# A transformer's attention output product computed by halves of the tokens, ahead of the next projection

## The chip, the cores and the metric
The kernel runs on one core of a Trainium2 chip. The metric is the device time of one execution in microseconds (us); lower is better. A core has TensorE (PE: matmuls; weight loads are shown apart as PEld), VectorE (DVE), ScalarE (ACT), GpSimd (POOL) and SyncE (SP), which here only starts DMAs. Each engine runs its own program in order; they meet at semaphores. PE writes its results to PSUM, which has eight banks of 128 x 512 fp32.

## What is computed
Four batches of 512 tokens, width 256, go through four blocks of gated cross-attention and feed-forward layers. The last of these feed-forward layers is itself a transformer of depth 6, and it alone is touched by the change:

```python
for i in range(DEPTH):          # 6
    x = attn_layer(shift_tokens(x), Wqkv[i], q_scale[i], k_scale[i], Wo[i]) + x
    x = ffn_layer(shift_tokens(x), ln_g[i], ln_b[i], W1[i], b1[i], W2[i], b2[i]) + x
```

`attn_layer` has 16 heads of 64: a projection to q, k and v, l2-normalized and rotated q and k, attention of each token to a window of 64 and the window before it, and the output product `out @ Wo`. `ffn_layer` is a layer norm, a product to two halves of 682, `a * gelu(gate)`, and a product back to 256.

## The kernel before
Before 2136 us the kernel computes the first parts (`first_part`), which the change leaves alone. `last_part` computes the transformer. x stays in SBUF, transposed: 2 chunks of 128 features by 4 batches by 512 tokens. A **unit** (d, g, b) is one layer d, one group g of four heads and one batch b: 96 units. Its 512 tokens are taken as four tiles tt of 128. fp32 values are split in a high and a low fp32r part, and every large product is three matmuls (`three`, L1449).

All engines walk the same list of steps, made by `last_order` (L1214). It puts steps into **turns**; unit n puts the steps of its tile tt at turn 4n + tt + lag, so that in a steady turn each stage works on another tile:
- `qkv` (lag 0, PE L1493): 12 matmuls, six of 512 columns (q, k) and six of 256 (v). DVE rotates q and k (L1631 to L1633), then ACT squares them (L1741); this Square is what frees the first PSUM bank of `qkv` (signal `sq_act`), the copy of v (L1738) the second.
- `rot` (lag 1): DVE sums the squares (L1639), POOL adds, clamps, takes a power and scales (L1814, L1816, L1818, L1821).
- `tr` (3, PE L1501) transposes q and k; ACT copies them (L1748, L1753).
- `sc`, `ex` (4): scores (PE L1511, L1516) into the one score buffer of two banks, maximum on DVE (L1645, L1649), four exps on ACT (L1760). The next `sc` waits until they are done.
- `dv` (5, DVE L1654, L1656), `pt` (6, PE L1525, ACT L1766), `pv` (7, PE L1535, ACT L1773 to `att_hi`, DVE L1660 to `att_lo`).
- `wo` m = 0, 1 (PE L1449 with wout, one per 128 output features: 6 matmuls of 512 columns each) at turns 4n + 10 and 4n + 11; `wx` (DVE L1666), which adds the product to x, both at 4n + 11.

Within a turn the order is that of `rank` and `place` (L1264 to L1271), the same for every engine; steps without a rank have 20, and among equals the order of `put` holds, units before FFN. For PE a turn reads `sc`, (`wo` m=1), `pv`, `tr`, `pt`, FFN steps, `qkv` (30), (`wo` m=0: 31). `lq` (32) loads, casts and splits weights (DVE L1615, POOL L1810).

The FFN of batch (d, b) is laid among the turns of later units: `fo` (POOL L1826: sum for the norm, waits for the last `wx`), `fa` (PE L1553, DVE L1672), `fq` (ACT L1778, POOL L1829), `fb` (PE L1558), `fy` (L1566), `fc`, `fd` (L1786, L1688), then `hg` (gate tiles, gelu L1794), `ha` and `hm` (linear tiles; DVE L1698 multiplies, L1705 casts to `hid_hi`, L1708 takes the rest of the half-filled last tile, POOL L1838 makes `hid_lo`) and `fw`, `fx` (back to 256). In turns with t mod 64 = 2, 18, 34 and 50 PE has `ha` of one batch and `fa` of another.

PSUM banks 2 to 7 are given out by `plan` (L84): it goes through the list of steps, takes for each step that needs a bank the one that has been free longest, and makes PE wait (`left`) for the signal that freed it. So the order of the list decides which signal a step waits for. The work buffers in SBUF (`work_at`) are handled likewise; in turns 50 to 52 the buffer of the rotary L1631 is one that POOL's L1838 or L1821 frees.

Of the kernel before, what the change touches and what calls it, by code (L numbers as in the profile page):

```python
# [7 lines left out]
ALU = mybir.AluOpType  # L8
# [9 lines left out]
P = 128  # L18
# [1195 lines left out]
def last_order():  # L1214
# [4 lines left out]
    def put(t, *parts):  # L1219
        turn.setdefault(t, []).extend(parts)  # L1220
# [17 lines left out]
    for n, (d, g, b) in enumerate(units):  # L1238
        for stage, lag in (("qkv", 0), ("mv", 1), ("rot", 1), ("tr", 3), ("sc", 4), ("ex", 4), ("dv", 5), ("pt", 6), ("pv", 7)):
            for tt in range(QT):  # L1240
                put(4 * n + tt + lag, (stage, (d, g, b, tt)))
        for m in range(C):
            put(4 * n + 10 + m, ("wo", (d, g, b, m)))
            put(4 * n + 11, ("wx", (d, g, b, m)))
    for d in range(DEPTH):
        for b in range(B):
            t0 = 64 * d + 32 * (b // 2)
# [13 lines left out]
            if d == DEPTH - 1:  # L1261
                put(t0 + second[0], ("kb", b))
                put(t0 + second[2] + 1, ("fin", b))
    rank = {st: i for i, st in enumerate(("fo", "mv", "sc", "wo", "pv", "tr", "rot", "dv", "ex", "pt", "wx"))}  # L1264
    rank.update({"qkv": 30, "lq": 32})

    def place(t, p):

        if t < 0:
            return 40 if p[0] not in rank else rank[p[0]]  # L1270
        return 31 if p[0] == "wo" and p[1][3] == 0 else rank.get(p[0], 20)  # L1271

    return Order(p for t in sorted(turn) for p in sorted(turn[t], key=lambda p: place(t, p)))

# [1 line left out]
def last_part(nc, a, at, s):  # L1276
# [14 lines left out]
    with ExitStack() as p2:  # L1291
# [78 lines left out]
        def remainder(u, i):  # L1370
# [5 lines left out]
        wqkv_at = plan(order, range(2), lambda p: [p[1][1:4]] if p[0] == "lq" and p[1][0] == "q" and p[1][4] == 0 else [],  # L1376
                       lambda p: [(w, "qkv_pe") for w, u in last_use.items() if p == ("qkv", u + (QT - 1,))])
        wout_at = plan(order, range(2), lambda p: [p[1][1:4]] if p[0] == "lq" and p[1][0] == "o" else [],
                       lambda p: [(w, "add_pe") for w, u in last_use.items() if p == ("wo", u + (C - 1,))])
        key_at = use(1, [("tr", 3, [(0,)], ["kT"])], [("sc", 3, [(QT - 1,)], ["kT"], "sc_pe")])  # L1380
        val_at = use(7, [("qkv", 4, any_, ["v"])], [("pv", 4, any_, ["v"], "pv_pe")])
        mix_at = plan(order, range(8),
# [37 lines left out]
        def bank(key):  # L1420
            return psum[:, one[key][0], :]
# [57 lines left out]
        def tensor_program():  # L1479
            PE.wait_ge(S_["rt_in"], 16 + 32)  # L1480
            PE.wait_ge(S_["zeroed"], 1)
            for stage, u in order.walk():
# [54 lines left out]
                                                    start=True, stop=True)  # L1537
                    ins.then_inc(S_["pv_pe"], 1)
                elif stage == "wo":
                    d, g, b, m = u  # L1540
                    PE.wait_ge(S_["pv_dve"], at_("pv", (d, g, b, QT - 1)))
                    w = weights_of(d, g, b)
                    PE.wait_ge(S_["lq_pool"], loaded(("o",) + w, 0))
                    wh, wl = wout_hi[:, wout_at[w][0], :], wout_lo[:, wout_at[w][0], :]
                    left(one, ("wo", u), PE)
                    for k in range(2):
                        w0 = k * D + m * P
                        ins = three(bank(("wo", u)), wh[:, w0:w0 + P], wl[:, w0:w0 + P], att_hi[:, k, :], att_lo[:, k, :], k == 0, k == 1)
                    ins.then_inc(S_["add_pe"], 1)
                elif stage == "fa":  # L1550
                    PE.wait_ge(S_["fo_pool"], at_("fo", u))
# [44 lines left out]
        def vector_program():  # L1596
# [3 lines left out]
            for stage, u in order.walk():  # L1600
# [59 lines left out]
                    vector.tensor_tensor(att_lo[:, :, tok(tt)], wide(bank(("pv", u, 0))[:, 0:2 * P]), att_hi[:, :, tok(tt)].bitcast(F32),  # L1660
                                         ALU.subtract).then_inc(S_["pv_dve"], 1)
                elif stage == "wx":
                    d, g, b, m = u
                    V.wait_ge(S_["add_pe"], at_("wo", u))
                    V.wait_ge(S_["xs_pool"], at_("xs", (d, b)))
                    vector.tensor_tensor(tokens(b, m), bank(("wo", u)), tokens(b, m), ALU.add).then_inc(S_["add_dve"], 1)  # L1666
                elif stage == "fa":
                    d, b = u
                    V.wait_ge(S_["fa_pe"], at_("fa", u))
# [52 lines left out]
        def scalar_program():  # L1722
            for stage, u in order.walk():
# [44 lines left out]
                elif stage == "pv":  # L1768
                    d, g, b, tt = u
                    A.wait_ge(S_["pv_pe"], at_("pv", u))  # L1770
                    if tt == 0 and (d, g, b) != (0, 0, 0):
                        A.wait_ge(S_["add_pe"], order.nth["wo", u[:3] + (0,)] - 1)
                    scalar.activation(att_hi[:, :, tok(tt)], wide(bank(("pv", u, 0))[:, 0:2 * P]), ACT.Copy).then_inc(S_["pv_act"], 1)  # L1773
                elif stage == "fq":
                    A.wait_ge(S_["fa_dve"], at_("fa", u))
                    left(work_at, ("n1", u), A)
                    for c in range(C):
                        ins = scalar.activation(buf(f"n{c}", u), buf(f"c{c}", u), ACT.Square)  # L1778
                    ins.then_inc(S_["fa_act"], 1)
                elif stage == "fc":  # L1780
                    d, b = u
                    A.wait_ge(S_["fy_dve"], at_("fy", u))
                    if batch_nth(u):
                        A.wait_ge(S_["ha_pe"], HT // 2 * batch_nth(u))
                    for c in range(C):
                        ins = scalar.activation(xn_hi[:, c, :], buf(f"c{c}", u), ACT.Identity, bias=vec(f"ln_b{d}", c))  # L1786
                    ins.then_inc(S_["fc_act"], 1)
                elif stage == "hg":
                    d, b, j = u
                    A.wait_ge(S_["hg_pe"], at_("hg", u))  # L1790
                    for i, key in zip(tiles_of(u), half_tiles(stage, u)):
                        r, lo = rows(i), P // 2 if i == HT - 1 else 0
                        left(work_at, ("g", (d, b), i), A)
                        ins = scalar.activation(buf("g", (d, b), i)[0:r, :], bank(key)[lo:lo + r, :], ACT.Gelu, bias=vec(f"b1g{d}", i)[lo:lo + r, :])  # L1794
                    ins.then_inc(S_["hg_act"], 1)

        def gpsimd_program():
            pool_step = at.pool_step
            G.wait_ge(S_["zeroed"], 1)
            for stage, u in order.walk():  # L1800
# [20 lines left out]
                    gpsimd.tensor_tensor(k, k, bc(st[:, 12:16], 2, LHD), ALU.mult).then_inc(S_["rot_pool"], 1)  # L1821
                elif stage == "fo":
                    d, b = u
                    G.wait_ge(S_["add_dve"], at_("wx", (d, last_group(b), b, C - 1)))
                    left(work_at, ("n0", u), G)
                    gpsimd.tensor_tensor(buf("n0", u), tokens(b, 0, 0), tokens(b, 1, 1), ALU.add).then_inc(S_["fo_pool"], 1)  # L1826
                elif stage == "fq":
# [246 lines left out]
```

## Time and profile before

| | us |
|---|---|
| median of 3 runs | 4802.01 (4800.52 to 4803.77) |
| profiled execution | 4805.08 |
| its span, first to last instruction | 4803.7 |
| PE busy | 4591.3 (96%) |
| DVE busy | 3584.6 (75%) |
| ACT busy | 3135.8 (65%) |
| POOL busy | 2594.6 (54%) |
| last part: first to last `sc` | 2136.0 to 4719.2 |

The page sums up one profiled execution. The timeline lists instructions in order of time; neighbours of one kind are merged (x4), the end of a matmul is modelled and overlaps its successor's start, so the length of PE's steps is read from start to start. In brackets stands the idle time of the engine before the instruction and who ended it. DVE and POOL instructions overlap their successors by some 0.08 us.

### The profile page before, as it was taken

How to read it: one execution, taken by the hardware profiler on the slowest of the kernel's cores; microseconds unless marked ns; L12 is line 12 of the kernel's file. 1: busy time of each engine (PE TensorE's matmuls, PEld its weight loads, DVE VectorE, ACT ScalarE, POOL GpSimd, SP SyncE). 2: the span in 40 equal slices, each digit the busy share in tenths (PEclk: the TensorE clock that was granted, in tenths of full speed). 3: DMA queues.
4: the chain of work that ended last, by engine and by line, in shares of the span. 5: the costliest groups of instructions: out<-in, count | busy, mean ns of one | idle time of the engine just before them, and what ended most of it. 6: DMA issues, size and time to landing. Idle time of an engine off the chain costs nothing.

```text
span 4803.7 us, 92378 instructions
## 1 busy us (share of the span) xinstructions
PE 4591.3 (96%) x34598; PEld 2927.6 (61%) x34664; DVE 3584.6 (75%) x6388; ACT 3135.8 (65%) x7744; POOL 2594.6 (54%) x2346
## 2 busy tenths in 40 slices
PE   6999999999999999969999999999999999999998
PEld 2333333334444343337788888888888888888886
DVE  4767766766675857858888887888888888887885
ACT  3666566556455556557777777777777777777773
POOL 3322211212121222148888788787888887887873
PEclk8999999999999999989999999999999999999999
DMA  5323323332222323212111111111111111111110
GB/s 121 66 50 62 75 42 60 71 63 47 57 40 60 68 41 74 40 34 54 41 41 35 41 40 36 42 39 37 39 44 39 39 36 41 40 36 38 39 44 31
DMA packets 178924, 233.05 MB, mean 49 GB/s; under 512 B 29648, under 2 KB 121424, under 8 KB 178256
## 3 DMA queue, kind: packets, MB, share of 16 engines
q1 hardware_dynamic: 178480, 227.14, 21.0%
q8 instruction: 277, 4.54, 0.4%
q14 instruction: 167, 1.37, 0.1%
HBM read 150.09 MB, written 32.51 MB: 38 GB/s over the span
## 4 chain that ended last, share of the span: by engine, by line
PE 66%; DVE 12%; ACT 8%; POOL 7%; issue 5%; DMA 1%; SPq 0%; another core or an unknown queue 0%; DVEq 0%; ACTq 0%; POOLq 0%
PE psum L1449 13%; PE psum L1493 11%; PE psum L541 5%; PE psum L527 5%; PE psum L506 5%; PE psum L1535 3%; PE psum L1501 3%; PE psum L488 2%; DVE maxes L731 2%; PE psum L1516 2%; PE psum L1525 2%; POOL stats L1818 2%; PE psum L530 2%; ACT lprobs L1760 2%; PE psum L496 2%
## 5 line engine op out<-in xcount | busy, mean ns | idle before, releaser
L941 ACT ACTIVATE probs<-psum 128x1024 f32<-128x1024 f32 x610 | 621.6, 1023 | 449.2 <-PE psum L527 259.7
L731 DVE TENSOR_REDUCE maxes<-psum 128x1 f32<-128x1024 f32 x512 | 618.1, 1216 | 278.0 <-PE psum L506 274.2
L1818 POOL TENSOR_TENSOR stats<-stats,minus_half 128x8 f32<-128x8 f32 x384 | 687.6, 1791 | 32.0
L1760 ACT ACTIVATE lprobs<-psum,small_stats,stats 128x128 f32<-128x128 f32 x1536 | 690.3, 480 | 20.9 <-DVE small_stats L1649 19.9
L1493 PE MATMUL psum<-wqkv_hi,xs_hi 128*128 128x512 f32 (+1 forms) x1536 | 546.6, 356 | 16.4 <-POOL xs_lo L1805 15.2
L1814 POOL TENSOR_TENSOR lwork<-lwork 128x512 f32<-128x512 f32 x384 | 505.1, 1315 | 74.7 <-DVE lwork L1633 74.6
L527 PE MATMUL psum<-stack 98*128 98x512 bf16 x1536 | 502.8, 384 | 25.9 <-DVE maxes L731 12.2
L1493 PE MATMUL psum<-wqkv_lo,xs_hi 128*128 128x512 f32 (+1 forms) x1536 | 519.3, 338 | 0.0
L1493 PE MATMUL psum<-wqkv_hi,xs_lo 128*128 128x512 f32 (+1 forms) x1536 | 519.0, 338 | 0.0
L506 PE MATMUL psum<-stack 96*128 96x512 bf16 x1536 | 473.3, 385 | 33.2 <-ACT probs L938 10.0
L728 DVE CUSTOM_DVE_ANT_0 psum<-psum,mask_by_query 128x1024 f32<-128x1024 f32 x256 | 314.8, 1231 | 217.8 <-PE psum L506 216.2
L1741 ACT ACTIVATE lwork<-psum 128x512 f32<-128x512 f32 x384 | 231.4, 603 | 358.0 <-DVE lwork L1633 357.9
L1631 DVE TENSOR_TENSOR lwork<-psum,rotary 128x512 f32<-128x512 f32 x384 | 262.5, 684 | 210.9 <-PE psum L1493 101.9
L541 PE MATMUL psum<-probs,values 128*32 128x512 f32 x3072 | 412.9, 610 | 0.8 <-ACT probs L941 0.8
L1656 DVE TENSOR_TENSOR lprobs<-lprobs,small_stats 128x512 f32<-128x512 f32 x384 | 380.0, 990 | 13.1
L527 PEld LDWEIGHTS psum<-stack 98*128 98x128 bf16 x1536 | 137.8, 100 | 390.0 <-issue 221.7
L1760 ACT ACTIVATION_READ_ACCUMULATOR lprobs<-psum,small_stats,stats 128x1 f32 x1536 | 348.9, 227 | 0.0
L1089 POOL TENSOR_TENSOR attn<-attn,sums 128x512 f32<-128x512 f32 x48 | 62.3, 1298 | 502.5 <-DVE sums L764 502.5
L1493 PEld LDWEIGHTS psum<-wqkv_hi,xs_hi 128*128 128x128 f32 x1536 | 291.4, 190 | 62.1 <-issue 20.9
L1493 PEld LDWEIGHTS psum<-wqkv_lo,xs_hi 128*128 128x128 f32 x1536 | 291.6, 190 | 43.7 <-issue 5.3
L1493 PEld LDWEIGHTS psum<-wqkv_hi,xs_lo 128*128 128x128 f32 x1536 | 290.8, 189 | 32.7
L506 PEld LDWEIGHTS psum<-stack 96*128 96x128 bf16 x1536 | 147.6, 98 | 261.6 <-ACT probs L938 27.8
(244 smaller groups left out, 11398.0 us busy)
## 6 DMA issues: line engine op xcount, KB each, us to landing
mixed_vals<-vals SPq DMA_DIRECT2D x672, 64.0 KB, 2.0
stack<-k_parts SPq DMA_DIRECT2D x288, 128.0 KB
staged<-in_quads SPq DMA_DIRECT2D x144, 256.0 KB, 3.0
k_parts<-parts SPq DMA_DIRECT2D x48, 384.0 KB, 2.9
stack<-q_parts SPq DMA_DIRECT2D x288, 64.0 KB
staged<-in_w SPq DMA_DIRECT2D x54, 256.0 KB, 3.0
ctx<-in_ctxT SPq DMA_DIRECT2D x24, 512.0 KB, 5.2
q_parts<-parts SPq DMA_DIRECT2D x24, 384.0 KB, 3.2
```

The lines of the kernel that those rows point to most:

```text
L506: ins = tensor.matmul(ps[:, i, :], q[0:STACK, h, qt * P:(qt + 1) * P], k[0:STACK, h, i * S:(i + 1) * S], start=True, stop=True)
L527: ins = tensor.matmul(ps[:, i, :], ky[0:STACK + 2, h, kt * P:(kt + 1) * P], q[0:STACK + 2, h, :], start=True, stop=L != 1)
L541: ins = tensor.matmul(bank(acc)[32 * h:32 * h + 32, :], values[:, kt, 4 * g + h, :], pr, start=kt == 0, stop=kt == KT - 1)
L728: ins = vector.tensor_tensor_reduce(out=scores, in0=scores, in1=masks_q[:, qt * S2:(qt + 1) * S2], scale=1.0, scalar=-3e38, op0=ALU.add, o ...
L731: ins = vector.tensor_reduce(to, pair(("M", u)), AX.XY, ALU.max)
L941: scalar.activation(probs[:, i % 6, :, :], pair(("E", u)), ACT.Exp).then_inc(S_["E_act"], 1)
L1449: ins = tensor.matmul(ps, l, r, start=first and n == 0, stop=last and n == 2)
L1493: ins = tensor.matmul(to, x_[:, c, b % 2, tok(tt)], w_[:, c * COLS + lo:c * COLS + hi], start=c == 0 and n == 0, stop=c == C - 1 and n == 2)
L1656: vector.tensor_tensor(pr, pr, bc(rc, 2, P), ALU.mult).then_inc(S_["dv_dve"], 1)
L1760: ins = scalar.activation(pr[:, h, :], scores(u)[:, h % 2, h // 2, :], ACT.Exp, bias=st[:, 4 + h:5 + h], scale=y[:, h:h + 1], accum_out=st ...
L1814: gpsimd.tensor_tensor(t1, t1, t2, ALU.add)
L1818: pool_step(gpsimd.tensor_tensor(st[:, 8:16], st[:, 0:8], minus_half[:, :], ALU.pow))
```

## The change
The output product of a unit is cut by tokens instead of by output features. `wo` of half 0 or 1 computes both 128-feature chunks for 256 tokens: 12 matmuls of 256 columns, into the two halves of one bank. Half 0 is put at turn 4n + 10, half 1 at 4n + 11, both without a rank (20), so between `pt` and `qkv`, ahead of the FFN's steps of the same turn. Each half is added to x one turn later (`wx` at 4n + 11 and 4n + 12), with one DVE instruction over both chunks. `wo` of half h waits for `pv` of tile 2h + 1 only; ACT, before it overwrites `att_hi` of tile 0 or 2, waits for `wo` of the half that it overwrites. `fo` moves from the first to the last rank of the ranked steps, since the last `wx` of a batch can now be in its turn.

```diff
@@ last_order
-        for m in range(C):
-            put(4 * n + 10 + m, ("wo", (d, g, b, m)))
-            put(4 * n + 11, ("wx", (d, g, b, m)))
+        for half in range(2):
+            put(4 * n + 10 + half, ("wo", (d, g, b, half)))
+            put(4 * n + 11 + half, ("wx", (d, g, b, half)))
...
-    rank = {st: i for i, st in enumerate(("fo", "mv", "sc", "wo", "pv", "tr", "rot", "dv", "ex", "pt", "wx"))}
+    rank = {st: i for i, st in enumerate(("mv", "sc", "pv", "tr", "rot", "dv", "ex", "pt", "wx", "fo"))}
...
-        return 31 if p[0] == "wo" and p[1][3] == 0 else rank.get(p[0], 20)
+        return rank.get(p[0], 20)
@@ tensor_program
                 elif stage == "wo":
-                    d, g, b, m = u
-                    PE.wait_ge(S_["pv_dve"], at_("pv", (d, g, b, QT - 1)))
+                    d, g, b, half = u
+                    PE.wait_ge(S_["pv_dve"], at_("pv", (d, g, b, 2 * half + 1)))
...
-                    for k in range(2):
-                        w0 = k * D + m * P
-                        ins = three(bank(("wo", u)), wh[:, w0:w0 + P], wl[:, w0:w0 + P], att_hi[:, k, :], att_lo[:, k, :], k == 0, k == 1)
+                    these = slice(2 * half * P, 2 * (half + 1) * P)
+                    for m in range(C):
+                        for k in range(2):
+                            w0 = k * D + m * P
+                            ins = three(bank(("wo", u))[:, 2 * m * P:2 * (m + 1) * P], wh[:, w0:w0 + P], wl[:, w0:w0 + P],
+                                        att_hi[:, k, these], att_lo[:, k, these], k == 0, k == 1)
@@ vector_program
-                    vector.tensor_tensor(tokens(b, m), bank(("wo", u)), tokens(b, m), ALU.add).then_inc(S_["add_dve"], 1)
+                    x = at.X[:, :, b, PAD + 2 * half * P:PAD + 2 * (half + 1) * P]
+                    vector.tensor_tensor(x, wide(bank(("wo", u))), x, ALU.add).then_inc(S_["add_dve"], 1)
@@ scalar_program
-                    if tt == 0 and (d, g, b) != (0, 0, 0):
-                        A.wait_ge(S_["add_pe"], order.nth["wo", u[:3] + (0,)] - 1)
+                    if tt % 2 == 0 and (d, g, b) != (0, 0, 0):
+                        A.wait_ge(S_["add_pe"], order.nth["wo", u[:3] + (tt // 2,)] - 2)
```

The release of the output weights and the wait of `fo` name the last half instead of the last chunk.

## Rows read from the trace of the kernel before

**Rows 1.** The page, its head and part 1: busy us, share, instructions
```profile
span 4803.7 us, 92378 instructions
...
PE 4591.3 (96%) x34598; PEld 2927.6 (61%) x34664; DVE 3584.6 (75%) x6388; ACT 3135.8 (65%) x7744; POOL 2594.6 (54%) x2346
```

**Rows 2.** The page, part 5: count, busy us, mean ns, idle before it
```profile
L1493 PEld LDWEIGHTS psum<-wqkv_hi,xs_hi 128*128 128x128 f32 x1536 | 291.4, 190 | 62.1 <-issue 20.9
```

**Rows 3.** Timeline of PE in two plain turns (42, 43): start us, length us
```profile
3039.71 0.30 PE L1511 MATMUL psum<-band_bias,ident_b 64*64 64x256 bf16 x4
...
3043.32 0.28 PE L1493 MATMUL psum<-wqkv_hi,xs_hi 128*128 128x256 f32 x1
3043.44 0.28 PE L1493 MATMUL psum<-wqkv_lo,xs_hi 128*128 128x256 f32 x1
...
3044.03 0.40 PE L1449 MATMUL psum<-att_hi,wout_hi 128*128 128x512 f32 x1
...
3045.20 0.39 PE L1449 MATMUL psum<-att_hi,wout_lo 128*128 128x512 f32 x1
3045.51 0.30 PE L1511 MATMUL psum<-band_bias,ident_b 64*64 64x256 bf16 x4
...
3046.18 0.50 PE L1449 MATMUL psum<-att_hi,wout_hi 128*128 128x512 f32 x1
...
3051.70 0.30 PE L1511 MATMUL psum<-band_bias,ident_b 64*64 64x256 bf16 x4
```

**Rows 4.** Timeline of ACT, end of turn 43: the last exp's read
```profile
3051.32 0.23 ACT L1760 ACTIVATION_READ_ACCUMULATOR lprobs<-psum,small_stats,stats 128x1 f32 x1
```

**Rows 5.** Timeline of PE: turn 48 (bound by PE) and turn 56
```profile
3271.24 0.30 PE L1511 MATMUL psum<-band_bias,ident_b 64*64 64x256 bf16 x4
...
3278.38 0.30 PE L1511 MATMUL psum<-band_bias,ident_b 64*64 64x256 bf16 x4
...
3328.18 0.30 PE L1511 MATMUL psum<-band_bias,ident_b 64*64 64x256 bf16 x4
...
3335.72 0.30 PE L1511 MATMUL psum<-band_bias,ident_b 64*64 64x256 bf16 x4
```

**Rows 6.** Timeline of PE in turns 50 to 52, up to turn 53's start
```profile
3285.86 0.30 PE L1511 MATMUL psum<-band_bias,ident_b 64*64 64x256 bf16 x4
...
3293.91 0.30 PE L1511 MATMUL psum<-band_bias,ident_b 64*64 64x256 bf16 x4
...
3300.10 0.30 PE L1511 MATMUL psum<-band_bias,ident_b 64*64 64x256 bf16 x4
...
3301.88 0.60 PE L1525 MATMUL psum<-ident,lprobs 128*128 128x128 f32 x4
...
3304.22 0.50 PE L1449 MATMUL psum<-hid_hi,w_hi 128*128 128x512 f32 x1 [0.57 <-ACT lwork L1741]
...
3308.81 0.30 PE L1511 MATMUL psum<-band_bias,ident_b 64*64 64x256 bf16 x4
```

**Rows 7.** Timeline of DVE, POOL and ACT in the same turns
```profile
3290.03 1.39 DVE L1698 SCALAR_TENSOR_TENSOR lwork<-psum,vecs,lwork 128x512 f32<-128x512 f32 x2
...
3292.22 1.07 POOL L1821 TENSOR_TENSOR lwork<-lwork,stats 128x256 f32<-128x256 f32 x1
...
3293.25 1.28 POOL L1838 TENSOR_TENSOR hid_lo<-lwork,hid_hi 128x512 fp32r<-128x512 f32 x1
3294.66 0.69 DVE L1631 TENSOR_TENSOR lwork<-psum,rotary 128x512 f32<-128x512 f32 x1 [0.53 <-POOL hid_lo L1838]
...
3296.05 0.60 ACT L1741 ACTIVATE lwork<-psum 128x512 f32<-128x512 f32 x1 [3.03 <-DVE lwork L1633]
...
3302.18 0.69 DVE L1631 TENSOR_TENSOR lwork<-psum,rotary 128x512 f32<-128x512 f32 x1 [1.48 <-POOL lwork L1821]
```

**Rows 8.** Timeline of POOL and DVE in turn 34
```profile
3622.21 1.46 POOL L1838 TENSOR_TENSOR hid_lo<-lwork,hid_hi 128x512 fp32r<-128x512 f32 x1
3622.56 1.66 DVE L1708 TENSOR_TENSOR hid_hi<-lwork,hid_hi 42x512 fp32r<-42x512 f32 x1
```

More of the change, by code:

```diff
@@ L1378, in last_part @@
         wout_at = plan(order, range(2), lambda p: [p[1][1:4]] if p[0] == "lq" and p[1][0] == "o" else [],
-                       lambda p: [(w, "add_pe") for w, u in last_use.items() if p == ("wo", u + (C - 1,))])
+                       lambda p: [(w, "add_pe") for w, u in last_use.items() if p == ("wo", u + (1,))])
         key_at = use(1, [("tr", 3, [(0,)], ["kT"])], [("sc", 3, [(QT - 1,)], ["kT"], "sc_pe")])
@@ L1662, in vector_program @@
                 elif stage == "wx":
-                    d, g, b, m = u
+                    d, g, b, half = u
                     V.wait_ge(S_["add_pe"], at_("wo", u))
                     V.wait_ge(S_["xs_pool"], at_("xs", (d, b)))
-                    vector.tensor_tensor(tokens(b, m), bank(("wo", u)), tokens(b, m), ALU.add).then_inc(S_["add_dve"], 1)
+                    x = at.X[:, :, b, PAD + 2 * half * P:PAD + 2 * (half + 1) * P]
+                    vector.tensor_tensor(x, wide(bank(("wo", u))), x, ALU.add).then_inc(S_["add_dve"], 1)
                 elif stage == "fa":
@@ L1823, in gpsimd_program @@
                     d, b = u
-                    G.wait_ge(S_["add_dve"], at_("wx", (d, last_group(b), b, C - 1)))
+                    G.wait_ge(S_["add_dve"], at_("wx", (d, last_group(b), b, 1)))
                     left(work_at, ("n0", u), G)
```

## Prediction

> **What bounds the kernel now.** I read the page first. TensorE (PE) is busy 96% of 4803.7 us, GpSimd (POOL), VectorE (DVE) and ScalarE (ACT) far less [rows 1]; that is a mean over two parts, and the change touches only the last one, from 2136 us on. So I went to the timeline of that part and cut it into turns at each first score matmul (L1511). There are 384 turns: `qkv` loads `wqkv_hi` weights four times a turn, 1536 times in all [rows 2]. I numbered each turn t as `last_order` does and name it by t mod 64; equal numbers recur once per layer and their lengths repeat within 0.03 us in the five full layers, so one stands for all.
>
> A unit (layer, head group, batch) touches two neighbouring turns with its output product, t mod 4 = 2 ("first": `wo` m=0, behind `qkv`) and 3 ("second": `wo` m=1, between `sc` and `pv`). Outside the FFN's ends all 72 first turns last 5.80 us and all 73 second ones 6.19, though both hold the same matmuls [rows 3]. In between the reader should see a PE that never rests: these turns are bound by PE's instruction stream. The rest of the layer has turns of 7.13 to 7.14 us when only PE binds [rows 5] and a few in which PE waits for another engine, and those decide this case.
>
> **Part 1: the product by halves.** Removed per unit: 12 matmuls of 512 columns. Added: 24 of 256 columns and 12 more weight loads. The six 512-column ones of `wo` start 1.17 / 5 = 0.234 us apart, the 256-column ones of `qkv` 0.12 (0.1185 over all six) [rows 3], each with its own load: 12 x 0.234 = 2.81 against 24 x 0.1185 = 2.84 us, +0.03 a unit: nothing. The load takes 0.19 us by itself [rows 2] but is hidden at this spacing. The Trainium skill, "TensorE: Matmul & The Clock Gate", Part 3, says that a weight load overlaps a running matmul only when the row groups differ; all loads here use all rows. By its figures (107 ns a load, 109 and 216 ns a matmul, an estimate) a unit would pay 24 x 216 - 12 x 323 = 1.3 us more, 125 us in all; the row speaks against it, since load and matmul together start every 118 ns.
> DVE's two additions stay 128x512 each, one per half; nothing is added to any DMA queue and SP's order is unchanged. The first addition comes a turn earlier relative to the second; both lie inside a DVE that waits in plain turns. Cost nothing; without cover 0.65 us each.
>
> **Part 2: second turns.** `wo` between `sc` and `pv` costs them twice. The stream restarts: 0.11 us at `wo`'s own start, about 0.09 before `pv`. And `pv` 1.4 us late makes all of ACT late: its last exp read ends 3051.55, and the next `sc`, which needs the one score buffer, starts only at 3051.70, 0.28 behind the last `qkv` matmul's slot instead of 0.09 [rows 3, 4]. Both go: `wo` behind `pt` joins the stream of `qkv`. What is late next is PE itself, so the second turn becomes as long as the first, 5.80. Gain 73 x 0.386 = 28.2 us. First turns keep 5.80: `wo` only swaps places with `qkv`.
>
> **Part 3: turns that wait because the second turn was late.** The ACT and DVE work of a second turn now ends over 1 us earlier and one addition leaves it. Turn 56 loses 0.40 us to a bank that the Square of the last `qkv` (L1741) frees, 7.54 against 7.14 [rows 5]. The same 0.4 stands in turns 9, 24, 25, 41, 57 (some behind the gelu's table load), 33 turns in all: 13.2 us. Turns 17 and 49 lose 0.33 (11 turns, 3.6), turn 33 0.16 (5, 0.8). I expect all gone: 17.6 us. In the first half of layer 0, without FFN, turns of 5.3 us wait likewise (estimate 3), and in the tail one half less stands between the last attention and the last norm: 6 x 0.234 = 1.4. Sum of parts 2 and 3: **50.2 us gained**, 40 to 55.
>
> **Part 4: the three turns at the end of each FFN.** Turns 50 to 52 (and 2 to 4, 18 to 20, 34 to 36; 21 triples) are bound by DVE and POOL. Two things get worse.
> (a) In turn 50 `wo` now stands ahead of `ha`, the FFN's last linear tile. `hm` on DVE (L1698) waits for `ha`: today it starts 4.17 us into the turn [rows 6, 7]. Then: `pt` ends 2.13, `wo` 1.49, five spacings 1.17, 0.51 to DVE: 5.3. Queued behind it on DVE are the casts, L1708, two L1672, and the rotary L1631.
> (b) The banks are dealt out first in, first out in program order. I followed that list through the old and the new order. In turn 51 it is `tr` (PE 2.9 us into the turn) that takes the bank freed by the last Square; now it is `pt`, due at 1.78. In turn 52 it is the second `fw` tile, due 3.4; now `pt` at 1.78. So everything behind `pt` (`wo`, `fw`, `fb`, `qkv`) waits for Square.
> Working, from the start of turn 50. L1698 runs 5.3 to 6.7. POOL's L1821 stands at 6.4, so the first cast ends at 7.3; the second holds DVE until 7.65; POOL's L1838, freed by the first cast, starts at 7.6 and takes 1.28 [rows 7]; L1708 comes behind it and is shut out until 8.8. That is what happens in turn 34 today: L1838 first, and L1708 takes 1.66 us, not 0.69 [rows 8]. The Trainium skill, "SBUF — State Buffer", Who interferes with whom, says so: an instruction with two SBUF inputs is fully blocked by a GpSimd one that started first. L1708 ends 9.45, the pair of L1672 10.7, L1631 starts 10.64 instead of 8.80. Square is done and seen by PE 2.05 later (1.39 + 0.60 + 0.06): `pt` goes at 12.69, which is 4.64 into turn 51; behind it 4.0 remain (0.36 + 1.49 + 2.16): turn 52 starts at 16.7, today 14.24 [rows 6]. The next L1631 follows 7.52 us behind the last as today, bound by POOL: 18.16; Square lets `pt` go at 20.21, 3.5 into turn 52. Behind `pt` today's turn has 8.71 - 1.78 - 0.74 (the wait that ends at 3304.22) = 6.2: turn 53 starts at 26.4, today 22.95. Cost 3.45.
> Eleven triples (18, 50) at 3.4, five (2, where `hm` is late already, at 4.6) at 3.3, five (34, no weight cast) at 2.7: **67 us lost**.
> Both ends: were DVE not late at all, (b) alone would cost 1.6, 1.6 and 1.4, 33 us; with `hm` late but L1708 ahead of L1838, L1631 starts at 9.55, a triple costs 2.2, 1.9 and 2.3, 45 us; with one more blocked operation a triple, 80. I take 67, because the order of requests that I work out is the one of rows 8.
> `fo` moves to the end of POOL's turn: it comes 4 us later, still before `fa` a turn on, and it lets `rot` go first. Nothing.
>
> **Sum.** 67.4 - 50.2 = +17.2 us. The profiled execution took 4805.08 us (span 4803.7): 4822.3. The median of the runs is 4802.01, 3.07 lower: **4819.2**. About 0.2%, 9.6 us, is what a measurement can tell from no change.
>
> **Rivals.** 1. Faster: PE's stream wins. If Square in turns 51 and 52 is not later than today, because DVE's and POOL's queues have slack that I don't see, only 33 us are lost and gains of up to 55 stand: 4780 to 4785. The place is L1631 of turn 50; it decides at a start of about 9.1 instead of 10.64. For it: plain turns are bound by PE without doubt. Against it: L1631 there waits for POOL today, and DVE has no idle time in that turn. Chance 0.25. 2. No change: `hm` is late but L1708 slips in ahead of L1838; 45 - 50 = -5: 4797. For it: the two requests lie within 0.1 us of each other in two of the four triples. Chance 0.2. 3. Weight loads show after all: 12 x 0.19 x 96 = up to 219 us, 4900 and more; rows 3 speak against it. Chance 0.02. 4. The change doesn't do what it says, since banks or PE order keep second turns long: no gain in part 2, 4845. Chance 0.05; the new order of PE reads straight from the code.
>
> **How the numbers follow.** My forecast, slower by 17, has 0.48. Range 4783 to 4842: the ends of the loss (33, 80) with the ends of the gain. Slower by over 9.6 us: 0.48 less its low edge, plus rivals 3 and 4: 0.52. Within: 0.23. Faster: 0.25. Slower and faster nearly balance, since the result is a difference of two sums of 50 to 70 us; the likeliest case alone spans 4808 to 4835.
>
> **What would show it.** Right: second turns of 5.8 us; 7.14 in turns 9, 24, 25, 56, 57; turns 51 and 52 of about 8.7 and 9.7 us where they were 6.19 and 8.71, with `pt` (L1525) released by ACT L1741 in both; L1698 of turn 50 at 5.3; L1708 near 1.7 us. Wrong: `pt` of turns 51, 52 near 1.8 us; `qkv`'s or `wo`'s 256-column spacing above 0.13; second turns still above 6.

## The result and the profile after

The changed kernel takes 4837.66 us, the median of 4 runs (4837.12 to 4839.79), against 4802.3 before: 1.0072 of the time, 95% interval 1.006 to 1.0084. It is slower by 35.4 us, where I had forecast 17.2. The time lies inside the range, near its upper end of 4842, the sign is right, and the forecast size is half of what came.

The head of the page of the changed kernel (busy us, share, instructions; compare [rows 1]):

```profile
span 4838.5 us, 94725 instructions
...
PE 4592.6 (95%) x35816; PEld 3028.4 (63%) x35816; DVE 3614.6 (75%) x6388; ACT 3165.8 (65%) x7744; POOL 2598.6 (54%) x2346
```

PE is busy 1.3 us longer and the span is 34.8 us longer: the loss is waiting, not work. Cutting both traces into turns at the first score matmul (L1511) shows where. Each row of this table is a sum over turns in us, worked out from the starts. Turns are named as in the prediction, by t mod 64; a "triple" is the three turns at the end of an FFN:

| turns | count | before | after | difference | forecast |
|---|---|---|---|---|---|
| the triples at the FFN's ends with the turn behind them (2 to 5, 18 to 21, 34 to 37, 50 to 53), from turn 50 of layer 0 on | 85 | 642.9 | 712.8 | +69.9 | +67.4 |
| 8 and 40 | 11 | 79.8 | 89.4 | +9.6 | 0 |
| second turns (t mod 4 = 3) | 65 | 402.1 | 381.7 | -20.4 | -25.1 |
| first turns (t mod 4 = 2) | 65 | 377.3 | 379.2 | +2.0 | 0 |
| other turns, 9, 24, 25, 41, 49, 56, 57 among them | 121 | 879.4 | 860.9 | -18.5 | -17.6 |
| before turn 40 of layer 0 | 36 | 201.7 | 197.2 | -4.5 | -6.1 |
| tail | | 84.6 | 81.2 | -3.4 | -1.4 |

(The forecast of 28.2 us for 73 second turns is split here: 65 x 0.386 = 25.1, and 3.1 with the 3 us for layer 0.)

PE in a second turn of the changed kernel (turn 43; start us, length us), which answers [rows 3]. `wo` is the stream that starts at 3253.23:

```profile
3251.09 0.30 PE L1511 MATMUL psum<-band_bias,ident_b 64*64 64x256 bf16 x4
...
3253.23 0.36 PE L1449 MATMUL psum<-att_hi,wout_hi 128*128 128x256 f32 x1
3253.43 0.28 PE L1449 MATMUL psum<-att_lo,wout_hi 128*128 128x256 f32 x1
...
3254.62 0.28 PE L1449 MATMUL psum<-att_hi,wout_lo 128*128 128x256 f32 x1
...
3256.93 0.30 PE L1511 MATMUL psum<-band_bias,ident_b 64*64 64x256 bf16 x4
```

The turn is 5.84 us long instead of 6.19. Behind the first, the matmuls of 256 columns start (3254.62 - 3253.43) / 10 = 0.119 us apart.

PE in turns 50 to 52 of the changed kernel, which answers [rows 6]; turn 51 starts at 3305.33, turn 52 at 3315.39:

```profile
3305.33 0.30 PE L1511 MATMUL psum<-band_bias,ident_b 64*64 64x256 bf16 x4
...
3308.20 0.63 PE L1501 MATMUL psum<-ident,lwork 128*128 128x128 f32 x4 [1.51 <-DVE lwork L1676]
3310.09 1.09 PE L1525 MATMUL psum<-ident,lprobs 128*128 128x128 f32 x4 [1.26 <-ACT lwork L1745]
...
3312.47 0.41 PE L1449 MATMUL psum<-att_lo,wout_hi 128*128 128x256 f32 x1
3312.68 0.35 PE L1449 MATMUL psum<-att_hi,wout_lo 128*128 128x256 f32 x1
...
3315.39 0.30 PE L1511 MATMUL psum<-band_bias,ident_b 64*64 64x256 bf16 x4
...
3317.58 0.63 PE L1525 MATMUL psum<-ident,lprobs 128*128 128x128 f32 x4 [0.26 <-ACT lwork L1745]
...
3323.68 0.30 PE L1511 MATMUL psum<-band_bias,ident_b 64*64 64x256 bf16 x4
```

`tr` (L1501) waits for the bank that L1676 frees, and `pt` (L1525) waits for the Square (L1745, before L1741) in both turns, as forecast. DVE and POOL beside it, turn 50's end, which answers [rows 7] (L1702, L1712, L1634, L1825, L1842 are L1698, L1708, L1631, L1821, L1838 of before):

```profile
3302.56 1.40 DVE L1702 SCALAR_TENSOR_TENSOR lwork<-psum,vecs,lwork 128x512 f32<-128x512 f32 x2 [0.98 <-PE psum L1449]
...
3305.09 1.65 DVE L1712 TENSOR_TENSOR hid_hi<-lwork,hid_hi 42x512 fp32r<-42x512 f32 x1
...
3307.97 0.69 DVE L1634 TENSOR_TENSOR lwork<-psum,rotary 128x512 f32<-128x512 f32 x1
```

```profile
3303.51 1.26 POOL L1825 TENSOR_TENSOR lwork<-lwork,stats 128x256 f32<-128x256 f32 x1
3304.74 1.45 POOL L1842 TENSOR_TENSOR hid_lo<-lwork,hid_hi 128x512 fp32r<-128x512 f32 x1
```

Turn 50 starts at 3297.25. L1702 comes 5.31 us into it, held up by PE; POOL's L1842 starts at 7.49, L1712 behind it at 7.84 and takes 1.65 us; L1634 starts at 10.72.

Turn 8 holds what I had not looked at. PE in turn 8 (start 3006.93), the first `hg` tile:

```profile
3006.93 0.30 PE L1511 MATMUL psum<-band_bias,ident_b 64*64 64x256 bf16 x4
...
3010.19 0.47 PE L1449 MATMUL psum<-xn_hi,w_hi 128*128 128x512 f32 x1 [0.88 <-ACT lwork L1745]
```

### The profile page after: what moved, and what is told of

It is laid out like the page before. It is cut to its first block, busy times and chain, and to the rows that moved or that the text cites. A ratio compares the mean times of both kernels' runs of the same rounds, so it can differ in the third digit from the quotient of the medians.

```text
span 4838.5 us, 94725 instructions
## 1 busy us (share of the span) xinstructions
PE 4592.6 (95%) x35816; PEld 3028.4 (63%) x35816; DVE 3614.6 (75%) x6388; ACT 3165.8 (65%) x7744; POOL 2598.6 (54%) x2346
## 4 chain that ended last, share of the span: by engine, by line
PE 71%; DVE 10%; POOL 9%; ACT 5%; issue 3%; DMA 1%; SPq 0%; DVEq 0%; ACTq 0%; POOLq 0%
PE psum L1449 14%; PE psum L1493 12%; PE psum L541 5%; PE psum L527 5%; PE psum L506 5%; PE psum L1535 3%; PE psum L1501 3%; PE psum L1525 3%; PE psum L1516 2%; PE psum L488 2%; DVE maxes L731 2%; POOL stats L1822 2%; PE psum L530 2%; PE psum L496 2%; POOL lwork L1818 2%
## 5 line engine op out<-in xcount | busy, mean ns | idle before, releaser
L1822 POOL TENSOR_TENSOR stats<-stats,minus_half 128x8 f32<-128x8 f32 x384 | 677.1, 1763 | 32.0
L1493 PE MATMUL psum<-wqkv_hi,xs_hi 128*128 128x512 f32 (+1 forms) x1536 | 535.2, 348 | 16.9 <-POOL xs_lo L1809 15.8
L1634 DVE TENSOR_TENSOR lwork<-psum,rotary 128x512 f32<-128x512 f32 x384 | 264.0, 688 | 311.1 <-PE psum L1493 256.6
L1745 ACT ACTIVATE lwork<-psum 128x512 f32<-128x512 f32 x384 | 229.9, 599 | 263.7 <-DVE lwork L1636 258.1
L1659 DVE TENSOR_TENSOR lprobs<-lprobs,small_stats 128x512 f32<-128x512 f32 x384 | 390.0, 1016 | 13.1
L1742 ACT ACTIVATE vals<-psum 128x256 f32<-128x256 f32 x384 | 149.2, 389 | 362.7 <-PE psum L1493 362.2
```

Of the source, the lines that this page charges most:

```text
L1493: ins = tensor.matmul(to, x_[:, c, b % 2, tok(tt)], w_[:, c * COLS + lo:c * COLS + hi], start=c == 0 and n == 0, stop=c == C - 1 and n == 2)
L1659: vector.tensor_tensor(pr, pr, bc(rc, 2, P), ALU.mult).then_inc(S_["dv_dve"], 1)
L1822: pool_step(gpsimd.tensor_tensor(st[:, 8:16], st[:, 0:8], minus_half[:, :], ALU.pow))
```

## The experiments

Ten kernels ran. Theory: the loss is made of two things that work together in turns 50 to 52, a late `hm` (part 4a) and the bank of the Square going to `pt` (4b), and the second one also makes turns 8 and 40 longer. Rivals: one of the two alone; DVE's and POOL's own chain; the cost of the 256-column matmuls. All times are medians; the ratio is to runs of the kernel before on the same chip, 4801.5 to 4806.0 us. A difference of two medians from different chips can therefore be off by up to 5 us; what a turn costs is compared within the traces.

**e1_swap: the other order of handing back.**

```diff
-            return [(p + (i,), sem) for i, sem in enumerate(LEAVES.get(stage, ()))]
+            return [(p + (i,), sem) for i, sem in reversed(list(enumerate(LEAVES.get(stage, ()))))]
```

> The changed kernel, with one thing else: `qkv`'s two PSUM banks are handed back in the other order, first the one that the copy of v (`qkv_act`) frees, then the one that the Square (`sq_act`) frees. Nothing is moved in any engine's program; only which bank a step gets, and so which signal it waits for. In turns 51 and 52 `pt` gets the bank of the copy, and `wo` (turn 51) or the second `fw` tile (turn 52) that of the Square; in turns 8 and 40 the first `hg` tile gets that of the copy. Theory (both the late `hm` and the dealing of the banks cost): turn 50's L1634 stays at 10.6 to 10.8 us, since `hm` is still late; in turn 51 `wo` waits in place of `pt`, 0.36 us less; turn 52 waits at `fw` as in the kernel before, so its end comes 4.6 us behind the Square instead of 6.2: a triple gets 1.6 us shorter, 21 x 1.6 = 34 us, and turns 8 and 40 go back to 7.13 or 7.17 us, 10 us: 4794 us (4785 to 4803). Rival A (the dealing alone costs): all 70 + 10 us come back, 4758. Rival B (DVE's and POOL's own chain sets the triples, whoever waits on PE): only turns 8 and 40 come back, 4828.

Measured: 4797.2 us, ratio 0.9987 (0.9979 to 0.9996). Turns 8 and 40 are 7.13 us again (-10.9 us over 11 turns), and the triples lose 41.0 us instead of 69.9. L1634 of turn 50 stays at 10.72 us. The theory's two terms are there; the triples gave back 28.9 us instead of 34. What is missing is in a few turns. PE in turn 19 and in turn 51 of this kernel, which hold the same steps:

```profile
3067.62 0.30 PE L1511 MATMUL psum<-band_bias,ident_b 64*64 64x256 bf16 x4
...
3070.48 0.63 PE L1501 MATMUL psum<-ident,lwork 128*128 128x128 f32 x4 [1.51 <-DVE lwork L1676]
...
3072.28 0.57 PE L1449 MATMUL psum<-att_hi,wout_hi 128*128 128x256 f32 x1 [0.73 <-ACT lwork L1745]
...
3073.08 0.41 PE L1449 MATMUL psum<-att_hi,wout_hi 128*128 128x256 f32 x1
3073.29 0.41 PE L1449 MATMUL psum<-att_lo,wout_hi 128*128 128x256 f32 x1
```

```profile
3290.65 0.63 PE L1501 MATMUL psum<-ident,lwork 128*128 128x128 f32 x4 [1.51 <-DVE lwork L1676]
...
3292.45 0.39 PE L1449 MATMUL psum<-att_hi,wout_hi 128*128 128x256 f32 x1 [0.73 <-ACT lwork L1745]
...
3293.26 0.28 PE L1449 MATMUL psum<-att_hi,wout_hi 128*128 128x256 f32 x1
3293.38 0.28 PE L1449 MATMUL psum<-att_lo,wout_hi 128*128 128x256 f32 x1
```

The busy times and the granted clock (the number behind POOL's) of those turns:

```profile
3067.60:3077.50 9.90, 7.66 (x69) 6.70 (x68) 7.97 (x14) 5.14 (x17) 6.20 (x6) 0.83 0.06 15
...
3287.80:3296.10 8.30, 6.06 (x69) 5.22 (x68) 7.96 (x14) 4.69 (x17) 4.68 (x5) 1.00 0.06 16
```

Both turns idle for 1.51 and 0.73 us, but in turn 19 the matmuls behind run at the lower clock level (1.2 GHz), 0.21 us apart instead of 0.12. Turn 19 takes 9.92 us, turn 51 8.39; the turns behind them, 7.87 and 8.41, take 0.54 of that back. So 1.0 us is lost here. Turn 19 does so in four of the five full layers (9.86 to 9.92 us) and in one not (8.39), turn 51 in none of six. Turn 35 does it in one layer, 9.50 us instead of 7.98, and nothing gives that back. Together this is 5 us, the gap between 34 and 28.9.

**e2_wo_behind_ffn: `wo` no longer ahead of `ha`.**

```diff
-    rank.update({"qkv": 30, "lq": 32})
+    rank.update({"wo": 21, "qkv": 30, "lq": 32})
```

> The changed kernel with `wo` at rank 21: behind the FFN's steps of its turn, ahead of `qkv`. The banks' dealing in turns 51 and 52 stays as in the changed kernel (`pt` gets the Square's). Theory: `ha` is computed 1.5 us earlier again, L1702 starts 4.17 us into turn 50 instead of 5.3, L1634 at 8.8 instead of 10.7, and only the loss that the banks bring is left, 1.6 us a triple instead of 3.4: 21 x 1.8 = 37 us come back, turns 8 and 40 (no `wo` in them) stay at 8.0 to 8.2: 4800 us (4792 to 4808). Rival A (the late `hm` has no part in it): 4838, L1634 may move but turn 51 stays above 10 us. Rival B (the late `hm` is all of it): 70 us come back, 4768.

Measured: 4801.0 us, 0.9994 (0.9985 to 1.0003), and the triples lose 35.2 us, half of 69.9. DVE in turn 50 (start 3281.91) of this kernel:

```profile
3286.17 1.39 DVE L1702 SCALAR_TENSOR_TENSOR lwork<-psum,vecs,lwork 128x512 f32<-128x512 f32 x2
...
3288.26 0.68 DVE L1712 TENSOR_TENSOR hid_hi<-lwork,hid_hi 42x512 fp32r<-42x512 f32 x1
...
3290.80 0.69 DVE L1634 TENSOR_TENSOR lwork<-psum,rotary 128x512 f32<-128x512 f32 x1 [0.53 <-POOL hid_lo L1842]
```

With `ha` ahead of `wo`, L1702 starts 4.26 us into the turn, L1712 takes 0.68 us again, and L1634 stands at 8.89. `pt` still waits for the Square, 0.99 us in turn 51, 1.50 in turn 52: turn 52 is 9.54 us. This is what the banks cost by themselves.

**e3_both: the two edits together.**

> Both edits together: `wo` behind the FFN's steps, and `qkv`'s banks handed back with the copy's first. Theory: L1634 of turn 50 at 8.8 us, the Square seen by PE at 10.85; in turn 51 `pt` is free to go, `wo` waits some 0.6 us for the Square; in turn 52 the second `fw` tile waits at 18.4 us as in the kernel before, so the triple is as long as there (22.95 us from 50 to 53). Turns 8 and 40 at 7.13 to 7.17. All of the 70 + 10 us come back and the 45 us gained elsewhere stay: 4758 us (4752 to 4766). If the two causes overlapped (each edit alone already brings all), e1 and e2 alone would stand there too. If the triples were lengthened by something else (the weight loads of the 256-column matmuls, the two additions of 128x512), this one would stay above 4790.

Measured: 4755.9 us, 0.9902 (0.9887 to 0.9917). The triples are 2.4 us longer than before instead of 69.9, turns 8 and 40 1.3 us shorter. The causes add up: e1 gives 40.4 us back, e2 36.6, both together 81.8. The 4.8 us more than the sum are about the 5 us that the clock takes in e1; in e3's trace the granted clock is full in all the triples. What is left of the waits (PE, turn 51 and turn 52):

```profile
3274.82 0.38 PE L1449 MATMUL psum<-att_hi,wout_hi 128*128 128x256 f32 x1 [0.46 <-ACT lwork L1745]
...
3282.34 0.50 PE L1449 MATMUL psum<-hid_hi,w_hi 128*128 128x512 f32 x1 [0.25 <-ACT lwork L1745]
```

**b_swap: the kernel before with e1's edit alone.**

> The kernel before, with `qkv`'s banks handed back in the other order and nothing else. It tests part 3: turns 9, 24, 25, 41, 56 and 57, 0.4 us longer than PE's own 7.13, wait for the Square's bank. If so, they fall to 7.13 to 7.17 us here too, with the second turns still 6.19: 33 x 0.4 = 13 us, and in turn 52 the second `fw` tile gets the copy's bank and `fb` the Square's, 0.57 us earlier x 21 = 12 us at most: 4785 us (4777 to 4791). If instead those turns wait because the second turn's ACT work is late, whatever the bank, nothing moves: 4802. e3 less this one is then what the output product by halves is worth by itself: second turns 20 to 28 us.

Measured: 4785.2 us, 0.9963 (0.995 to 0.9975), the time forecast, but not wholly from where it was forecast. Turns 17, 24, 33, 49 and 56 fall to 7.13 or 7.14; turns 9, 25, 41 and 57 do not (7.61, 7.93, 7.59, 7.93 in most layers; 25 and 57 had been 7.54): PE in turn 57 waits at `pt` for the bank of the gelu, which stands behind its table load on ACT. PE there:

```profile
3326.58 0.63 PE L1525 MATMUL psum<-ident,lprobs 128*128 128x128 f32 x4 [0.60 <-ACT lwork L1794]
```

So part 3's turns waited for two things: some for the Square's bank (the swap frees them), some for a late ACT (the swap does not help, and the change does: 7.13 in all four). The triples became 14.7 us shorter than in the kernel before, and part 3's turns only 3.0: the sum of 4785 came out by luck. With the same handing back on both sides, the output product by halves behind the FFN's steps (e3) is worth 4785.2 - 4755.9 = 29.3 us.

**e4_rest_first: DVE's L1712 and POOL's L1842 never together.**

```diff
+                            if i == HT - 2:
+                                G.wait_ge(S_["rest_dve"], batch_nth(u) + 1)
```

> The changed kernel with one wait more: for a batch's last pair of tiles POOL starts L1842 only when DVE's L1712 is done, so the two never run together. `hm` stays late, the banks are dealt as in the changed kernel. Theory (of the 1.8 us by which L1634 is late in turn 50, 1.1 come from `ha` behind `wo`, the rest from L1712 being shut out by L1842): L1712 takes 0.69 us instead of 1.65 and ends at 8.3, L1842 runs 8.4 to 9.7, L1634 starts at 9.7 instead of 10.7; a triple gets 1.0 us shorter, 21 us in all: 4816 us (4808 to 4822). Rival A (the shutting out costs nothing, since L1634 waits for a work buffer in any case): 4838 or, as L1842 itself comes later, up to 4845. Rival B (the price of the changed kernel is mostly this shutting out): under 4800.

Measured: 4823.5 us, 1.0046 (1.0032 to 1.0059): 14 us of the 35 come back, fewer than the 21 expected and above the range's end. DVE and POOL in turns 50 and 51 (50 starts at 3289.66):

```profile
3297.50 0.69 DVE L1712 TENSOR_TENSOR hid_hi<-lwork,hid_hi 42x512 fp32r<-42x512 f32 x1
...
3299.74 0.69 DVE L1634 TENSOR_TENSOR lwork<-psum,rotary 128x512 f32<-128x512 f32 x1 [0.24 <-POOL hid_lo L1844]
```

```profile
3298.33 1.27 POOL L1844 TENSOR_TENSOR hid_lo<-lwork,hid_hi 128x512 fp32r<-128x512 f32 x1 [1.15 <-DVE hid_hi L1712]
```

L1712 takes 0.69 us instead of 1.65, 0.96 less, but L1634 is only 0.64 us earlier (10.08 into turn 50), since now it waits 0.24 us for the work buffer that POOL frees. L1634 stood at 8.89 in e2, so the changed kernel has it 1.83 us late. At least 0.64 of that, 0.64 x 21 = 13 us, is the shutting out, and at most 1.19 a triple comes from `ha` alone; e4's own wait makes POOL later, so it does not divide the two exactly.

**e5_cols256 and e9_cols128: the cut alone, in the old places.**

```diff
-                    for k in range(2):
+                    for c in range(0, 4 * P, 256):          # e9: 128
+                        for k in range(2):
...
+                            ins = three(bank(("wo", u))[:, c:c + 256], wh[:, w0:w0 + P], wl[:, w0:w0 + P],
+                                        att_hi[:, k, c:c + 256], att_lo[:, k, c:c + 256], k == 0, k == 1)
```

> The kernel before with each of `wo`'s matmuls of 512 columns cut in two of 256, in the old places (between `sc` and `pv`, and behind `qkv`): 24 matmuls and 24 weight loads a unit instead of 12 and 12, nothing moved. It measures part 1 alone. By the spacing of rows 3 (0.1185 against 0.234 us): 96 x 0.03 = 3 us more, 4805 (4801 to 4810). By the rule that a load is not hidden behind a matmul on the same rows, 1.3 us a unit: 4927.

> As e5, with `wo`'s matmuls cut in four of 128 columns, 48 matmuls and 48 weight loads a unit, in the old places. It asks at what length of a matmul a weight load can no longer be hidden. If the spacing keeps falling with the columns (0.234, 0.118, then 0.06 us), the turns stay within 0.1 us of e5's and the kernel within 10 us of it: 4813 to 4823. If the load sets a floor between the 0.10 us and the 0.19 us that one takes, a unit pays 48 x (0.10 to 0.19) - 2.8 = 2.0 to 6.3 us more: 4990 to 5400 us.

e5 measured 4813.0 us, 1.0023 (1.0013 to 1.0033): 11.5 us more, not 3 and above my range, and not 125. First turns are 0.05 us longer and second ones 0.03, so a unit pays 0.08 us for 12 more matmuls, 7.7 us in all. Another 6.2 come in turns 8 and 40; in turn 40 it is a race described below. e9 measured 5031.7 us, 1.047 (1.0452 to 1.0487). PE in the second turn of e9, four of the 24 matmuls:

```profile
3334.60 0.28 PE L1449 MATMUL psum<-att_hi,wout_hi 128*128 128x128 f32 x1
3334.71 0.28 PE L1449 MATMUL psum<-att_lo,wout_hi 128*128 128x128 f32 x1
3334.82 0.27 PE L1449 MATMUL psum<-att_hi,wout_lo 128*128 128x128 f32 x1
3334.94 0.27 PE L1449 MATMUL psum<-att_hi,wout_hi 128*128 128x128 f32 x1
```

They start 0.111 us apart, half the columns of e5 at nearly the same spacing (0.119). So a matmul with its own weight load takes at least 0.11 us here, however short, and of the three lengths tried 256 columns is the shortest that wastes nothing: 48 x 0.111 - 12 x 0.234 = 2.5 us a unit, 242 us, and 226 were measured. That the load sets this floor, and not the matmul itself, is likely and not shown: no run has 128-column matmuls of this kind without loads.

**e6_features_behind_pt: the move without the cut.**

```diff
-            put(4 * n + 11, ("wx", (d, g, b, m)))
+            put(4 * n + 11 + m, ("wx", (d, g, b, m)))
...
-        return 31 if p[0] == "wo" and p[1][3] == 0 else rank.get(p[0], 20)
+        return rank.get(p[0], 20)
```

`wo` also loses its rank and `fo` moves to the end, as in the change.

> The move without the cut: `wo` still by output features, each over all 512 tokens, but placed as in the changed kernel, behind `pt` in turns 4n + 10 and 4n + 11, with each addition one turn later. The copy of `pv`'s tile 0 on ACT overwrites tokens that the second product still reads, so it waits for that product, which now stands behind `pt`: it goes at 3.9 us into the second turn instead of 2.4, and behind it on ACT stand the copies of `tr` and the four exps on which the next `sc` waits. Theory: second turns of 6.19 + 1.5 = 7.7 us, 73 x 1.5 = 107 us, and the triples lose 70 as in the changed kernel: 4980 us (4940 to 5050). Rival (the place is what counts and the cut by tokens brings nothing): second turns of 5.8 to 5.9, 4838 us.

Measured: 5037.1 us, 1.0491 (1.0477 to 1.0506). Without the cut the move costs 235 us, so the cut is needed. The time lies in my range by luck: I had 107 us in second turns and 70 in the triples, and measured are 38 in second turns, 79 in first ones and 100 in the triples. PE in the first turn 14 (start 3115.85) and the start of turn 16, and ACT in the second turn 15 (start 3125.23):

```profile
3119.97 0.51 PE L1449 MATMUL psum<-att_hi,wout_hi 128*128 128x512 f32 x1 [1.75 <-DVE att_lo L1660]
...
3131.99 0.30 PE L1511 MATMUL psum<-band_bias,ident_b 64*64 64x256 bf16 x3 [0.91 <-ACT lprobs L1760]
```

```profile
3129.10 0.38 ACT L1773 ACTIVATE att_hi<-psum 128x256 fp32r<-128x256 f32 x1 [2.50 <-PE psum L1449]
```

In second turns ACT's copy waits for the product, as expected, at 3.87 us; they last 6.77 us, not 7.7 (0.58 more each). One reason is that in the kernel before that copy starts at 2.99 us (turn 43, start 3045.51), not at 2.4 as I had taken it:

```profile
3048.50 0.39 ACT L1773 ACTIVATE att_hi<-psum 128x256 fp32r<-128x256 f32 x1 [0.78 <-PE psum L1535]
```

In first turns, which I had left at 5.8, `wo` m=0 needs all four tiles of the unit, and the last of them is subtracted by DVE in this very turn: the 65 first turns are 79 us longer. Most of them last 6.0 to 7.8 us; turn 14 shown here is one of four at 9.4, in which the granted clock also fell to its lower level. A half needs only tiles that were ready a turn or more ago.

**e8_late_rot and e10_wx_same_turn: can the rest be had?**

e8, on top of e2's edit:

```diff
-            return [(p + (i,), sem) for i, sem in enumerate(LEAVES.get(stage, ()))]
+            if stage == "qkv":
+                return [(p + (1,), "qkv_act")]
+            gone = [(p + (i,), sem) for i, sem in enumerate(LEAVES.get(stage, ()))]
+            if stage == "rot":
+                gone.append((("qkv", u, 0), ("sq_act", order.nth["qkv", u])))
+            return gone
```

> `wo` behind the FFN's steps as in e3, and the planner told that the Square's bank comes late: the copy's bank is handed back at `qkv`, the Square's only at `rot`, a turn on. In turn 51 `wo` then gets the bank of `pv` and in turn 52 the second `fw` tile that of `pv`, so that only `qkv` itself, 3 us later, gets the Square's. Theory (e3's triples still lose the waits for the Square, 0.74 us in turn 51 and 0.5 in turn 52; b_swap's triple shows 7.87 for turn 52): turn 51 falls from 6.57 to 5.83, turn 52 from 8.39 to 7.87, 21 x 1.25 = 26 us: 4730 us (4726 to 4742). Rival (DVE's and POOL's work of the triple, 22.4 us or more, is the bound, and any wait removed at PE comes back as another, at `tr` or at the rotary): 4750 or more.

Measured: 4776.8 us, 0.9949 (0.9935 to 0.9962), 21 us slower than e3. `wo` in turn 51 (start 3282.39) now waits for the bank of `pv`, and goes at 3.43 us into the turn, where e3's goes at 2.84:

```profile
3285.82 0.39 PE L1454 MATMUL psum<-att_hi,wout_hi 128*128 128x256 f32 x1 [1.05 <-DVE att_lo L1668]
```

The rival was right: in these turns DVE is full, and a bank that DVE frees is no better than the Square's. What helps is one more bank, which is e10's way. Its edit on top of e3:

```diff
-            put(4 * n + 11 + half, ("wx", (d, g, b, half)))
+            put(4 * n + 10 + half, ("wx", (d, g, b, half)))
...
-    rank.update({"wo": 21, "qkv": 30, "lq": 32})
+    rank.update({"wo": 21, "wx": 22, "qkv": 30, "lq": 32})
```

> e3 with each half added in the turn that computes it: `wx` of half 0 at 4n + 10, of half 1 at 4n + 11, ranked right behind `wo` and ahead of `qkv`. The product's bank is then handed back before the turn ends instead of a turn later, so one bank more is free when the next turn deals: in turn 51 `pt` gets the addition's, `wo` the copy's, and only `qkv` the Square's; in turn 52 the second `fw` tile gets the copy's and `fb` the Square's, as in b_swap. Theory: the waits for the Square in turns 51 and 52 go, 0.73 and 0.52 us, so 21 x 1.25 = 26 us less than e3: 4730 us (4725 to 4740). Rival: the addition of half 0, now ahead of the rotary in turn 50 on a DVE that is full there, makes L1634 and with it the whole chain up to 0.65 us later, and half of the gain is lost again: 4742 to 4750.

Measured: 4746.2 us, 0.9875 (0.986 to 0.989), the fastest kernel here: 59.9 us below the kernel before on its chip. Turns 51 and 52 are 5.83 and 7.87 us, the waits are gone and the triples 22 us shorter than e3's. It misses 4730 mainly because turn 40 (7.77) and turn 41 (8.07) grew, 8 us in five layers: in turn 39 an addition now stands behind `fd` on DVE. This side effect was read from the timeline and not tried. The time falls in the rival's range, but the rival fails where it was placed, since L1634 of turn 50 stands at 8.81. It holds in turn 34 alone, where L1634 starts at 9.91 instead of e3's 9.31, and the turns behind it give 0.4 us instead of 1.25.

## Why the prediction was right in sign and half in size

**Part 1, the cut costs nothing: nearly.** I forecast 0.03 us a unit. First turns became 0.03 longer, second ones end at 5.833 instead of 5.803, so it is 0.06 a unit, 0.08 in e5: 6 to 8 us instead of 3, on a sum of 17. The term that was mis-sized is 12 x 0.234 against 24 x 0.1185. Taken from the unrounded starts, the 512-column matmuls of `wo` in turn 42 of the kernel before are 0.232 us apart (1.161 / 5), and those of 256 columns in the changed kernel 0.1187: 24 x 0.1187 - 12 x 0.232 = 0.065 us. The weighing of the rule on row groups held: no load of 0.1 us is added to each matmul (125 us were not paid). The runs show more than the row did: load and matmul overlap, but e9's floor of 0.11 us stands right under the 0.119 of 256 columns. The same page of the Trainium skill, "TensorE: Matmul & The Clock Gate", in its section "LDWEIGHTS (loading the stationary operand)", gives 107 ns for a load of 128 columns. The 0.111 of e9 agrees with that figure. It does not agree with the sentence of Part 3 that load and matmul overlap only when the row groups differ, and here the measurement decides. (Part 3 also names loads into a background weight buffer as pulled ahead of running matmuls; no row here tells whether that happens.)

**Part 2, second turns: mechanism right, 2.5 us small.** 5.83 to 5.95 instead of 5.80. Turns 7, 11, 15, 27, 39, 47 and 59 kept 0.03 to 0.12 us because `wo` had been dealt the Square's bank there too; e1 takes them all to 5.833.

**Part 3, turns that waited: right.** 18.5 us against 17.6, all at 7.133. b_swap adds that they had two causes. The tail gave 3.4 instead of 1.4.

**Part 4, the triples: right in sum and mechanism, wrong in the split.** 69.9 against 67.4; L1702 at 5.31 (5.3), L1712 1.65 us (1.66), L1634 at 10.72 (10.64), `pt` of turn 52 at 20.33 us from turn 50's start (20.21). e2, e1 and e4 confirm the two causes and the shutting out one by one. Turn 51 took 10.05 us, not 8.7, and turn 52 8.29, not 9.7. The step that failed is "behind it 4.0 remain" for the stretch from `pt` to the end of turn 51: it measured 5.30 us (3310.09 to 3315.39). PE idles twice in turn 51, 1.51 and 1.26 us, and `pt` and nine matmuls of `wo` behind it run at the lower clock level; that is why they start 0.21 us apart. In most triples this costs nothing, and two of them show it. In turn 51 of layer 0 (and 19 of layer 4) the granted clock stayed full:

```profile
2408.54 0.30 PE L1511 MATMUL psum<-band_bias,ident_b 64*64 64x256 bf16 x4
...
2413.30 0.63 PE L1525 MATMUL psum<-ident,lprobs 128*128 128x128 f32 x4 [1.26 <-ACT lwork L1745]
...
2417.39 0.30 PE L1511 MATMUL psum<-band_bias,ident_b 64*64 64x256 bf16 x4
...
2420.81 0.63 PE L1525 MATMUL psum<-ident,lprobs 128*128 128x128 f32 x4 [1.48 <-ACT lwork L1745]
...
2426.91 0.30 PE L1511 MATMUL psum<-band_bias,ident_b 64*64 64x256 bf16 x4
```

Here 4.09 us lie between `pt` and the end of turn 51, turns 51 and 52 are 8.85 and 9.53 us, much as forecast, and their sum, 18.4, is the same as at the lower clock (10.05 + 8.29 = 18.3). What PE loses by the clock it would else have waited for the Square, and the Square's time is set by DVE and POOL. So the clock is not what made the changed kernel slower. In three triples of the 21 the lower level lasts longer, turn 51 (or 3, or 19) grows to 11.45 to 11.51 us, and the sum of the two turns is 19.3 us instead of 18.4; these 3 us cover what 69.9 has over 67.4.

**What was missed: turns 8 and 40, 9.6 us.** In the kernel before, the first `hg` tile of these turns gets a bank that an addition frees, the second the Square's. With both additions no longer in one turn, every later step moves up by one bank: the first `hg` tile gets the Square's, and waits 0.88 us in turn 8 and 0.67 in turn 40. I had followed the list of banks through turns 50 to 52 only. It is the same rule as in part 4b, and following it through all 64 turns would have put 11 x 0.9 = 10 us on the sum. e1 shows it: the same turns at 7.13.

So the missing 18 us are 9.6 for turns 8 and 40, 6.7 in the first and second turns (the cut and bank waits), 2.5 in the triples and 1.6 before turn 40 of layer 0, less the 2.9 that the other turns and the tail gave more.

**Rivals.** Rival 1 (the Square isn't later) fails at the point it named, L1634 at 10.72 and not 9.1. Rival 2 (L1712 slips in ahead of L1842) fails in this kernel, and e2 shows that it happens as soon as `hm` is on time. Rivals 3 and 4 fail: no 200 us of loads, and second turns did fall.

## What to carry to other kernels

Where a planner deals out banks in the order of the program, a moved step, or one that holds its bank longer, shifts the bank of every step behind it. List for the whole period, before and after, which signal each step gets, and look for steps that now get the one that comes last. Then ask which resource is handed back late only in the list: here the order of two words in a tuple was worth 18 us in the kernel before, and 81.8 us of the changed kernel's time hung on that and a rank.

## What the runs showed of the hardware

**Two operations on DVE and POOL shut each other out, and a lead of 0.02 to 0.05 us decides who.** In turn 39 of the kernel before DVE starts its product of the probabilities at 3216.65 and POOL its sum at 3216.70:

```profile
3216.65 0.69 DVE L1656 TENSOR_TENSOR lprobs<-lprobs,small_stats 128x512 f32<-128x512 f32 x1
```

```profile
3216.70 1.79 POOL L1814 TENSOR_TENSOR lwork<-lwork 128x512 f32<-128x512 f32 x1
```

In e5 the same pair comes the other way round:

```profile
3218.03 1.82 DVE L1658 TENSOR_TENSOR lprobs<-lprobs,small_stats 128x512 f32<-128x512 f32 x1
```

```profile
3218.01 1.29 POOL L1816 TENSOR_TENSOR lwork<-lwork 128x512 f32<-128x512 f32 x1
```

Who starts first takes its usual time (0.69 and 1.29 us), the other 0.5 to 1.1 us more. In e5 both additions slip into turn 40 for that, and turn 40 takes 8.30 us instead of 7.16. Measured from the start of the turn, DVE's operation is 0.04 us later and POOL's 0.03 earlier than in the kernel before. So small a shift cost 1.1 us in each of the five full layers.

**Idle PE and its clock.** After the same two idles, of 1.51 and 0.73 us, the granted clock fell in turn 19 of e1 in four layers of five and stayed full in turn 51 in all six. What tells the two apart is not in these rows and stays open.
